# Attention with split weights: low and high parts contiguous per block of keys, one 512-column matmul for both, and VectorE's order changed

## The reference

```python
xn = layernorm(x)                                  # x: 1 x 2048 x 256
q, k, v = split(einsum('bsd,ed->bse', xn, Wqkv))   # 16 heads of 128 each
w = softmax(einsum('bqhd,bkhd->bhqk', q, k) * 128 ** -0.5)
attn = einsum('bse,de->bsd', einsum('bhqk,bkhd->bqhd', w, v), Wout)
ffn = (sigmoid(xn @ Q(w1).T) * (xn @ Q(w2).T)) @ Q(w3).T   # Q: to -1, 0, 1
out = x + attn + ffn
```

## Time and profile before

| | |
|---|---|
| Median of 3 runs | 1956.21 us (1951.72 to 1957.82) |
| Profiled execution, own time | 1959.55 us |
| Its span, first to last instruction | 1957.7 us |
| TensorE busy (matmul) | 97% of the span |
| VectorE / ScalarE / GpSimd busy | 82% / 64% / 69% |
| Granted TensorE clock, mean | 0.994 of full speed |
| DMA | 302.45 MB, 154 GB/s |

### The profile page before, as it was taken

The page is one execution under the profiler, slowest core; times in us unless marked ns, Lnnn a source line. Parts: engine busy times, 40 slices in busy tenths (PEclk is TensorE's granted clock), DMA queues, the critical chain, the costliest instruction groups (busy, mean ns, idle before and its releaser), DMA issues.

```text
span 1957.7 us, 33299 instructions
## 1 busy us (share of the span) xinstructions
PE 1894.0 (97%) x11556; PEld 1694.3 (87%) x11556; DVE 1599.0 (82%) x2088; ACT 1251.4 (64%) x1698; POOL 1355.2 (69%) x514
## 2 busy tenths in 40 slices
PE   5979999999999999999999999999999999999997
PEld 4859898998888899888888989888998889889886
DVE  6378888888888888888888888788888888888883
ACT  3446676666666676666667666666766667666663
POOL 2417676776767677676767777676776767687676
PEclk9999999999999999999999999999999999999998
DMA  3046667676767767676776767677676767767675
GB/s 104 1 104 153 161 162 175 151 177 157 165 144 166 175 149 175 159 165 143 169 175 148 174 159 168 142 170 175 148 177 159 163 156 165 177 146 175 146 166 136
DMA packets 197241, 302.45 MB, mean 154 GB/s; under 512 B 38144, under 2 KB 57280, under 8 KB 197056
## 3 DMA queue, kind: packets, MB, share of 16 engines
q1 hardware_dynamic: 197056, 300.11, 65.6%
HBM read 12.65 MB, written 2.10 MB: 8 GB/s over the span
## 4 chain that ended last, share of the span: by engine, by line
PE 59%; POOL 13%; issue 11%; SPq 9%; DVE 3%; ACT 2%; DMA 2%; POOLq 0%; DVEq 0%; ACTq 0%
POOL pt L975 11%; SPq L257 8%; PE ps_o L354 8%; PE ps_o L356 8%; PE ps_o L355 8%; PE ps_s L342 7%; PE ps_s L344 7%; PE ps_s L343 7%; PE ps_t L332 3%; PE ps_s L313 3%; PE ps_t L322 3%; DMA pt<-prob 2%; PE ps_s L388 2%; DVE prob L840 1%; POOL v_lo L966 1%
## 5 line engine op out<-in xcount | busy, mean ns | idle before, releaser
L975 POOL TENSOR_TENSOR pt<-pt,pt_hi 128x2048 fp32r<-128x2048 f32 x256 | 1181.4, 4615 | 477.6 <-ACT pt_hi L621 476.3
L629 ACT ACTIVATE prob<-ps_s,neg_max 128x1024 f32<-128x1024 f32 x512 | 566.9, 1114 | 467.0 <-DVE neg_max L831 466.9
L840 DVE STREAM_TRANSPOSE prob<-prob 128x1024 f32<-128x1024 f32 x512 | 612.8, 1232 | 162.9 <-ACT prob L629 162.9
L827 DVE TENSOR_REDUCE row_max<-ps_s 128x1 f32<-128x1024 f32 x512 | 619.8, 1215 | 65.7 <-PE ps_s L344 36.3
L354 PE MATMUL ps_o<-pt_hi,v_hi 128*128 128x256 f32 x2048 | 583.8, 285 | 13.5 <-POOL v_lo L966 6.8
L356 PE MATMUL ps_o<-pt_hi,v_lo 128*128 128x256 f32 x2048 | 582.6, 284 | 0.0
L355 PE MATMUL ps_o<-pt,v_hi 128*128 128x256 f32 x2048 | 580.6, 284 | 0.0
L621 ACT CAST pt_hi<-pt 128x2048 fp32r<-128x2048 f32 x256 | 491.1, 1919 | 137.5 <-DMA pt<-prob 130.9
L342 PE MATMUL ps_s<-k_hi,q_hi 128*128 128x512 f32 x1024 | 403.9, 394 | 22.8 <-ACT prob L629 17.3
L354 PEld LDWEIGHTS ps_o<-pt_hi,v_hi 128*128 128x128 f32 x2048 | 388.1, 189 | 22.5 <-POOL pt L975 7.2
L344 PE MATMUL ps_s<-k_hi,q_lo 128*128 128x512 f32 x1024 | 401.1, 392 | 0.0
(11 more groups left out here) (95 smaller groups left out, 1667.8 us busy)
## 6 DMA issues: line engine op xcount, KB each, us to landing
pt<-prob SPq DMA_DIRECT2D x2048, 128.0 KB, 2.4
v_raw<-v_turned SPq DMA_DIRECT2D x244, 64.0 KB, 2.0
w_raw<-wqkv_dram SPq DMA_DIRECT2D x32, 128.0 KB, 2.5
y<-x_dram SPq DMA_DIRECT2D x4, 512.0 KB, 5.6
wo_raw<-wqkv_dram SPq DMA_DIRECT2D x16, 128.0 KB, 2.5
wo_raw<-wo_dram SPq DMA_DIRECT2D x16, 128.0 KB, 2.2
out_dram<-y SPq DMA_DIRECT2D x8, 256.0 KB, 2.9
w_raw<-w_dram SPq DMA_DIRECT2D x2, 704.0 KB, 8.8
```

The costliest lines, as they stand in the source:

```text
L629: nc.scalar.activation(prob[:, t % E_RING, half * HALF:(half + 1) * HALF], ps_s[:, 2 * half:2 * half + 2, :].rearrange("p b n -> p (b n)") ...
L827: nc.vector.reduce_max(row_max[:, t, half:half + 1], ps_s[:, 2 * half:2 * half + 2, :].rearrange("p b n -> p (b n)"), AX_X).then_inc(s_mx, 1)
L840: nc.vector.transpose(tile, tile).then_inc(s_xp, 1)
L975: nc.gpsimd.tensor_tensor(raw, raw.bitcast(F32), pt_hi.rearrange("p t (i x) -> p (t i) x", i=4)[:, :, col], ALU.subtract).then_inc(s_pl, 1)
```

## The change

- The weights of a pair are kept in `parts`, laid out per block of keys: 256 columns of the low part, then 256 of the high part, contiguous. ScalarE writes the high, GpSimd the low part there, in runs of 32 columns; the moved blocks land in `raw`, a ring of two pairs.
- Per block of keys one matmul of 512 columns multiplies the high values with low and high weights at once (into both halves of the bank `ps_pv`), and one of 256 columns adds the low values by the high weights to the high half.
- `output_low` on VectorE is two operations, the second waiting for the first.
- VectorE turns the second half of an even tile in the odd tile behind it; both halves of a `result` stand in the even tile, behind `inverse`.
- The wait for a free place in the ring is no longer VectorE's (for products three pairs back) but the DMA queue's, ahead of a pair's moves (for the subtraction two pairs back).
- Since the ring no longer comes round after three heads, the loop's body on four engines is one head (`Fori(1, H - 2)`, heads 1 to 13); on SyncE all 16 heads are written out.

```diff
-RAW_RING = 3
+RAW_RING = 2
...
-        pt = sb("pt", [P, RAW_RING, 2, S], F32R)
-        pt_hi = sb("pt_hi", [P, 2, S], F32R)
+        raw = sb("raw", [P, RAW_RING, 2, S])
+        parts = sb("parts", [P, T, 2, 8, BLK], F32R)
...
+        def moved(p, half):
+            return raw[:, p % RAW_RING].rearrange("p t (i b q) -> p (t i) b q", i=4, q=BLK)[
+                :, :, half * KH:(half + 1) * KH, :]
+        def half_of(which, half):
+            return parts[:, half * KH:(half + 1) * KH, which].rearrange("p b a q -> p a b q")
...
                 for p in range(PAIRS):
                     sp.wait_ge(s_xp, count(32, h, 4 * p + 4))
+                    if h[0] or p >= RAW_RING:
+                        sp.wait_ge(s_pl, count(16, h, 2 * (p - RAW_RING) + 2))
                     move(h, p, 0)
...
-            head((0, 0, 0), 9)
-            with sp.Fori(1, H - 5, RAW_RING) as it:
-                for n in range(RAW_RING):
-                    head((it, n, (n + 1) % RAW_RING), 9)
-            for n in (3, 2, 1):
-                head((H - n, 0, (H - n) % RAW_RING), n - 1)
+            for n in range(H):
+                head((n, 0), H - 1 - n)
...
-                    nc.tensor.matmul(dst, v_hi[:, kb, :], hi[:, :, col], start=(kb == 0), stop=False)
-                    nc.tensor.matmul(dst, v_hi[:, kb, :], lo[:, :, col], start=False, stop=False)
-                    last = nc.tensor.matmul(dst, v_lo[:, kb, :], hi[:, :, col], start=False, stop=(kb == T - 1))
+                    nc.tensor.matmul(ps_pv, v_hi[:, kb, :], parts[:, kb].rearrange("p s a q -> p (s a q)"),
+                                     start=(kb == 0), stop=False, skip_group_check=True)
+                    last = nc.tensor.matmul(ps_pv_hi, v_lo[:, kb, :], parts[:, kb, 1].rearrange("p a q -> p (a q)"),
+                                            start=False, stop=(kb == T - 1), skip_group_check=True)
...
-            head((0, 0, 0), True, False)
-            with pe.Fori(1, H - 5, RAW_RING) as it:
-                for n in range(RAW_RING):
-                    head((it, n, (n + 1) % RAW_RING), False, False)
-            for n in (3, 2, 1):
-                head((H - n, 0, (H - n) % RAW_RING), False, n == 1)
+            head((0, 0), True, False)
+            with pe.Fori(1, H - 2) as it:
+                head((it, 0), False, False)
+            for n in (2, 1):
+                head((H - n, 0), False, n == 1)
...
-                nc.scalar.copy(pt_hi.rearrange("p t (i x) -> p (t i) x", i=4)[:, :, col],
-                               pt[:, slot(h, p)].rearrange("p t (i x) -> p (t i) x", i=4)[:, :, col].bitcast(F32)
-                               ).then_inc(s_ph, 1)
+                nc.scalar.copy(half_of(1, half), moved(p, half)).then_inc(s_ph, 1)
...
-                if t % 2 and half and reused:
-                    dve.wait_ge(s_pv, count(16, h, 2 * (t // 2 - RAW_RING) + 2))
...
-                nc.vector.tensor_tensor(o_lo[:], ps_pv, o_hi[:], ALU.subtract).then_inc(s_olo, 1)
+                nc.vector.tensor_tensor(o_lo[:], ps_pv_hi, o_hi[:], ALU.subtract).then_inc(s_orest, 1)
+                dve.wait_ge(s_orest, count(8, h, p + 1))
+                nc.vector.tensor_tensor(o_lo[:], ps_pv_lo, o_lo[:].bitcast(F32), ALU.add).then_inc(s_olo, 1)
...
-                    turn(h, t, 0, False)
-                    turn(h, t, 1, not first or t >= 2 * RAW_RING)
+                    if t % 2:
+                        turn(h, t - 1, 1)
+                    turn(h, t, 0)
+                    if t % 2:
+                        turn(h, t, 1)
...
-                nc.gpsimd.tensor_tensor(raw, raw.bitcast(F32),
-                                        pt_hi.rearrange("p t (i x) -> p (t i) x", i=4)[:, :, col],
-                                        ALU.subtract).then_inc(s_pl, 1)
+                nc.gpsimd.tensor_tensor(half_of(0, half), moved(p, half), half_of(1, half), ALU.subtract
+                                        ).then_inc(s_pl, 1)
```

More of the change, by code:

```diff
@@ L927, in _ @@
                 output_low(end, p)
[L928 to L929 removed]
+                result(end, p)
         @block.gpsimd
```

112 lines of the change are left out of this document (48 added, 64 removed).

## The result

The changed kernel takes **1926.09 us** (median of 4 runs, 1924.72 to 1927.86), the kernel before 1954.81 beside it (4 runs, 1951.72 to 1957.82): a ratio of 0.9854 (95% interval 0.9834 to 0.9873). The profiled execution took 1927.86 us, with a span of 1926.0 and a granted clock of 0.994, as before.

What follows compares the result with a forecast made beforehand. TensorE's own issue rate was taken as the bound. Products -22, handoffs +10, tail +1, three returns -11.7 and twelve returns +23 summed to 0: 1956.5 us, no change; own range 1948 to 1965, overall 1930 to 1976.

Steps and rivals of the forecast that it cites:

- What bounds the kernel: Whole kernel: TensorE's own issue rate is the bound, busy 97% of the span; other engines run in its shadow.
- Products, -22: TensorE's products: one 512- and one 256-column matmul replace three of 256, 0.349 against 0.360 us a block, -22 us.
- contiguity itself brings between 0 and 4 us: TensorE's products: reading contiguous instead of strided columns saves 0 to 4 us; taken as 0.
- rival C: TensorE's products: the 512-column matmul does not run at 0.229 us alternating with a 256-column one; 1978 us, chance 4%.
- ScalarE and GpSimd, 0: High copy and subtraction writing 32-column runs: 0 to 0.2 us more per subtraction, taken as 0, covered by GpSimd's idle time.
- VectorE, in its shadow with 0.3 us to spare: VectorE's loop per pair of tiles: closes at 12.87 us against TensorE's 13.18, so no direct cost.
- Rival B: VectorE becomes the bound, in the odd tile: 1972 us, range 1965 to 1985, chance 21%.
- Handoffs, +10: Handoffs to TensorE: 0.8 us less slack makes products wait for v_lo and logits for k_lo; 0 to 15, taken +10 us.
- Tail, +1: End of the kernel: second low operation three times in series and the later turn cost +1 us.
- Three returns gone, -11.7: Old three-head loop: its three returns, 3.9 us each, disappear, -11.7 us.
- Twelve returns, +23: New one-head loop on four engines: twelve returns at 1.9 us each, +23 us.
- rival A: New one-head loop: the shorter body returns for free, 1934 us, 1929 to 1940 with handoffs; chance 27%.

Runs made afterwards that it cites:

- the strided kernel with three matmuls: Changed kernel with three 256-column matmuls per key block and split weights strided as before the change: 1937.94 us, ratio 0.9933.
- the split projection: Changed kernel with three 256-column matmuls per block, and half of the output projection ahead of each half's products: 1914.04 us, ratio 0.9793.
- the run written out: Kernel before the change with all 16 heads written out on all five engines, no loop return: 1939.0 us, ratio 0.9927.

## Why the prediction was wrong

Two terms failed: the twelve returns, put at +23 us, cost 0; and contiguous operands, put at 0, brought 21 to 24, of which the joined matmul lost 9.5. The gain, by ratios to the kernel before: loops, order and ring -0.7% (13 us, the strided kernel with three matmuls), contiguous operands -1.2% (24), joined matmul +0.4% (9).

- **What bounds the kernel**: right. TensorE was the bound before and after, and the gain is its work and its waits.
- **Products, -22**: failed, in two places that partly hid each other; the sum came to -15. The step "contiguity itself brings between 0 and 4 us" was the wrong one: it brings 21 to 24. Its price was read from the output projection, 0.118 us a matmul with contiguous columns, and that is the projection's own price, 0.120 even right behind products that run at 0.1175. The products' contiguous prices, 0.1142 and 0.1175, stood nowhere in the trace of before. Why the projection takes longer stays open. The other step, a joined matmul at the logits' 0.229 beside one at 0.120, missed that joining leaves every step at 2.82 us: where the forecast had a saving of 22, joining on contiguous operands costs 9.5. The two matmuls take 0.235 and 0.118 us in the middle of a step (rival C's mechanism, given 4%, behind a gain that covers it). By the formula of the Trainium skill ("TensorE: Matmul & The Clock Gate", section "Wait — 56ns, not 53.3ns?") the estimate of the saving is 2.5 ns a block, not the prediction's 2.6. The Trainium skill ("Advanced Engine Details and Errata", section "SBUF Cachelines") speaks of a penalty only where accesses do not share a 16-byte line; read so, runs of 32 fp32 columns would cost no more than contiguous ones. Here they cost 0.1200 against 0.1142 to 0.1175 us a matmul; the measurement decides.
- **ScalarE and GpSimd, 0**: right. The subtraction with runs of 32 columns on the output takes 4631 ns, against 4615.
- **VectorE, in its shadow with 0.3 us to spare**: right in that no wait came, and to 0.04 us in the step that was followed; the rest of the loop was not measured against it. Rival B did not come.
- **Handoffs, +10**: failed; the term was 0. "0.8 us less slack" holds for the one head it was read from, v_lo 0.84 to 0.14, by luck. Most heads had at most 0.26 us before and should have waited; they have 0.06 to 0.23 after. What kept the 0.8 from them stays open. The margin is thin all the same: three-head bodies, written-out code and the split projection each push v_lo over it, for 0.2 to 1.2 us in the heads concerned. **Tail, +1**: from the last head's start to the end it is 138.8 us after, 140.5 before, the faster product steps included; the term by itself was not measured.
- **Three returns gone, -11.7**: right in kind, 14 by the run written out. The queue's share was put at 2.0 and measured 2.4; the rest at 1.9, measured 1.5.
- **Twelve returns, +23**: the step that failed by most. It carried the price of a return from a three-head body over to a one-head body, "from the part that stays". It measured 0, and rival A (27%) had it, with 1934 us; at 111.55 us, the heads are even under the 112.2 it gave, by the better products. VectorE's 2.96 us of idle time comes with the three-head body and goes with the one-head body. The Trainium skill ("Runtime: NRT & Kernel Launch", section "Instruction fetch mechanics") gives TensorE room for 2048 instructions, 512 for other engines. One head is 570 matmuls and 569 weight loads there and 133 timed instructions on VectorE, so by that figure both fit; three heads overflow TensorE's. I had held TensorE to the two blocks of 256. The trace agrees with the larger room: q8 has 20 packets against 101, and none of the 20 starts between 314 and 1675 us, while the loop runs. With the instructions counted that only wait, VectorE's head has the "some 190" of the prediction, and three heads some 570, over that figure's 512. This is why a short body can return for free, but not all of it: in the changed kernel TensorE's code is loaded all along with a three-head body too, and its return shows no idle time. What made its idle time at the return in the kernel before stays open.

## What to carry to other kernels

Read a price only from rows of the same kind: a matmul's distance depended on its operand's runs, on which product it belongs to and on what ran just ahead. Read a slack from every head and not from one. Joining two matmuls into a wider one isn't a saving by itself; count steps of 8 blocks before and after, and try the layout without the joining. A loop's return is priced by the size of its body: try a shorter one before writing it all out, and look at the packets of both instruction queues. Many packets tell that a body is loaded anew, not that it costs time.

## What was not expected of the hardware

- A run of 24 matmuls of 256 contiguous columns has two paces, 0.1142 and 0.1175 us each, at a granted clock of 1.00 (the 2.4 GHz level), and keeps it from about its sixth matmul to its end. Where TensorE does not wait it is nearly always fast behind the output projection and slow behind logits; a wait of 0.1 us at the start can bring either. Places of weights and values, the order of the loads, and GpSimd's work don't change it. What in the engine keeps the pace stays open.
- Moving operands in 8 runs of 32 columns hold every step at 0.120, whatever runs ahead.
- A loop of one head, returning twelve times, was no slower than the same program written out (1926.09 against 1929.57 us).
